# Values ahead of the turned z, and a half K tile with high and low halves one above the other

## What is computed

```python
q = (x @ Wq).reshape(b, t, h, dh).transpose(0, 2, 1, 3)      # h = 8 heads, dh = 64
k = (x @ Wk).reshape(b, t, h, dh).transpose(0, 2, 1, 3)
gl_v = (x @ Ws).reshape(b, t, h, e)                          # e = 5 experts, 2 selected
wv = _topk_mask(gl_v, SEL) * jax.nn.sigmoid(gl_v)
xv = jnp.einsum('btd,edk->btek', x, Wv)
v = jnp.einsum('bthe,btek->bhtk', wv, xv)
scores = jnp.einsum('bhid,bhjd->bhij', q * scale, k)
probs = jax.nn.softmax(scores, axis=-1)
attn = jnp.einsum('bhij,bhjd->bihd', probs, v)
mask_o = _topk_mask((x @ Wd).reshape(b, t, h, e), SEL)
out = jnp.einsum('bthe,bthk,ekd->btd', mask_o, attn, Wo)
...
x = x + jnp.tanh(g_ffn[0]) * _L0_ffn_ref(_layernorm(x, axis=-1), ...)
```

## Time and profile before

| what | us |
|---|---|
| median of 3 runs | 1264.33 (1263.65 to 1264.37) |
| the profiled execution | 1264.03 |
| its span, first to last instruction | 1262.2 |
| PE matmul busy | 1215.5 (96%), 6376 instructions |
| PE weight loads busy | 907.1 (72%) |
| DVE busy | 835.8 (66%) |
| POOL busy | 663.0 (53%) |
| ACT busy | 648.2 (51%) |

### The profile page before, as it was taken

One profiled execution on the slowest core, in us unless ns is written; L12 is line 12 of the kernel. 1 busy time (PEld: TensorE's weight loads), 2 busy tenths in 40 slices (PEclk: granted clock), 3 DMA queues, 4 the chain that ended last, 5 costly groups with the idle time before them and its releaser, 6 DMA issues.

```text
span 1262.2 us, 19742 instructions
## 1 busy us (share of the span) xinstructions
PE 1215.5 (96%) x6376; PEld 907.1 (72%) x6376; DVE 835.8 (66%) x1526; ACT 648.2 (51%) x1423; POOL 663.0 (53%) x481
## 2 busy tenths in 40 slices
PE   5899999999999999999999999999999999999995
PEld 4688888888888888766666766767667677676654
DVE  7777777778686947464675665765755756657654
ACT  6434343434343434375556656656656655665551
POOL 2724242424243433377495594692791872963971
PEclk9899999999999999999999999999999999999998
DMA  6231314132222314300011010010010020010010
GB/s 217 100 126 42 125 42 125 63 104 79 88 91 85 104 57 146 105 1 34 1 35 66 0 66 33 0 66 33 0 66 33 0 70 30 7 59 0 17 50 34
DMA packets 40666, 75.74 MB, mean 60 GB/s; under 512 B 3712, under 2 KB 4224, under 8 KB 40640
## 3 DMA queue, kind: packets, MB, share of 16 engines
q1 hardware_dynamic: 40640, 75.42, 17.5%
HBM read 58.63 MB, written 16.78 MB: 60 GB/s over the span
## 4 chain that ended last, share of the span: by engine, by line
PE 86%; DVE 7%; POOL 3%; issue 2%; ACT 1%; DMA 0%; DVEq 0%; SPq 0%; ACTq 0%; POOLq 0%
PE ps_f L878 20%; PE ps_r L1745 11%; PE ps_o L1819 9%; PE ps_s L1806 8%; PE ps_h L878 7%; PE ps_s L1798 7%; PE ps_s L878 7%; PE ps_r L1781 5%; PE ps_r L1757 5%; DVE z L1526 2%; POOL spare L1323 2%; POOL spare L1329 2%; DVE z_tmp L1515 1%; PE ps_t L912 1%; PE ps_r L1771 1%
## 5 line engine op out<-in xcount | busy, mean ns | idle before, releaser
L1341 POOL TENSOR_TENSOR z<-z,z_tmp 128x1280 f32<-128x1280 f32 x40 | 117.0, 2926 | 200.1 <-DVE z_tmp L1515 198.0
L1495 DVE TENSOR_REDUCE nmax<-ps_s 128x1 f32<-128x512 f32 x256 | 163.9, 682 | 85.1 <-PE ps_s L1798 84.0
L1389 ACT ACTIVATE pt<-ps_s 128x512 f32<-128x512 f32 x256 | 139.3, 596 | 144.7 <-PE ps_s L1806 144.4
L1323 POOL TENSOR_TENSOR spare<-xv,pick 128x512 f32<-128x512 f32 x160 | 176.0, 1100 | 41.8 <-DVE pick L1608 28.7
L1380 ACT ACTIVATE tmp<-ps_s,nmax 128x512 f32<-128x512 f32 x256 | 174.4, 694 | 15.6 <-DVE nmax L1495 15.6
L1329 POOL TENSOR_TENSOR spare<-spare 128x512 f32<-128x512 f32 x128 | 172.4, 1347 | 10.0
L1806 PEld LDWEIGHTS ps_s<-ident,tmp 128*128 128x128 f32 x1024 | 109.5, 140 | 48.5 <-issue 40.5
L1806 PE MATMUL ps_s<-ident,tmp 128*128 128x128 f32 x1024 | 140.4, 280 | 1.3 <-ACT tmp L1380 1.3
L1798 PE MATMUL ps_s<-k,q 64*128 64x512 f32 x768 | 123.5, 426 | 3.7 <-ACT pt L1389 3.7
L1819 PE MATMUL ps_o<-pt,spare 128*64 128x512 f32 x512 | 116.9, 598 | 0.7 <-ACT pt L1389 0.7
L255 POOL TENSOR_TENSOR e_t<-e_t 128x512 fp32r<-128x512 f32 x32 | 40.8, 1302 | 142.4 <-ACT e_t L474 142.4
(11 more groups left out here) (181 smaller groups left out, 2122.2 us busy)
## 6 DMA issues: line engine op xcount, KB each, us to landing
stage<-in_x SPq DMA_DIRECT2D x32, 256.0 KB, 3.1
x_sb<-in_x SPq DMA_DIRECT2D x8, 1024.0 KB, 5.4
x_dram<-x_sb SPq DMA_DIRECT2D x32, 256.0 KB, 2.4
stage<-x_dram SPq DMA_DIRECT2D x8, 1024.0 KB, 5.8
x_sb<-x_dram SPq DMA_DIRECT2D x8, 1024.0 KB, 5.7
out_dram<-x_sb SPq DMA_DIRECT2D x32, 256.0 KB, 2.0
stage<-in_ctx_t SPq DMA_DIRECT2D x28, 256.0 KB, 3.1
stage<-in_ctx SPq DMA_DIRECT2D x28, 256.0 KB, 2.7
```

The source lines that it names most:

```text
L1323: pool.tensor_tensor(v_tmp[:] if e else acc, xv[:, :, e, :].unsqueeze(2).broadcast_to(shape), pick[:, 0, e, :, 2 * p:2 * p + 2].unsqueeze( ...
L1341: pool.tensor_tensor(zv, zv, z_tmp[:, h % 2], ALU.add).then_inc(z_pool, 1)
L1389: act.activation(pt[:, h % 4, :, t * P:(t + 1) * P], ps_s[:, n % BANKS, :].rearrange("p (k t) -> p k t", k=NT), ACT.Copy).then_inc(pt_read ...
L1495: dve.tensor_reduce(nmax[:, n:n + 1], ps_s[:, n % BANKS, :], AX_X, ALU.max, negate=True).then_inc(nmax_ready, 1)
```

## The change

Two things. First, PE's shared parts move from part 2 of a step to a new part 3, so that the values of both batches come before the shared parts of both. Second, z gets 384 columns: ACT copies its last 64 columns behind themselves (`copy_last`), so the third turned tile holds the same 64 values twice, in rows 0 to 63 and in rows 64 to 127. ACT writes the whole tile as the high half into `z_t2[:, 1]`; DVE then turns rows 64 to 127 into low halves, in place. The weights' third tile holds the high half in both places, and in its low tile the low half above zeros. So two matmuls take the place of three. Result tile 0 waits for each low half just ahead of its passes.

```diff
+    LAST = KZ - 1
+    HALF = NV - LAST * P
+    assert 2 * HALF == P
...
+        z_all = sb("z", [P, NT, KZ * P])
+        z = z_all[:, :, 0:NV]
...
-            for k in range(KZ):
-                into = passing("wo", k)
-                sp.dma_start(into, wo[k * P:k * P + into.shape[0], :]).then_inc(wo_loaded[k], 16)
+            for k in range(LAST):
+                sp.dma_start(passing("wo", 0, k), wo[k * P:(k + 1) * P, :]).then_inc(wo_loaded[k], 16)
+            for place in (0, HALF):
+                sp.dma_start(wo_raw[place:place + HALF, LAST, :], wo[LAST * P:NV, :]).then_inc(wo_loaded[LAST], 16)
...
-            pool.memset(wo2[0:SHARED, :, KZ - 1, :].bitcast(F32), 0.0).then_inc(cleared, 1)
+            pool.wait_ge(cleared, 1)
+            pool.memset(wo2[HALF:P, 1, LAST, :].bitcast(F32), 0.0).then_inc(cleared, 1)
+            pool.wait_ge(cleared, 2)
...
-                    act.activation(z_t2[:, 0, n, :], ps, ACT.Copy).then_inc(zt_hi, 1)
+                    act.activation(z_t2[:, int(n == LAST), n, :], ps, ACT.Copy).then_inc(zt_hi, 1)
+
+            def copy_last(b):
+
+                act.wait_ge(z_ready, b * 2 + 2)
+                act.activation(z_all[:, :, NV:KZ * P], z_all[:, :, NV - HALF:NV], ACT.Copy).then_inc(z_copied, 1)
...
+                        if n == TURN_Z_AT[0] - STEPS and not first:
+                            copy_last(b - 1)
                         for tile in (n, n + 1):
                             if 0 <= tile < STEPS:
                                 scores_exp(b, tile, first)
...
-                    dve.tensor_tensor(z_t2[:, 1, n, :], ps, z_t2[:, 0, n, :].bitcast(F32),
+
+                    rows, high = (slice(HALF, P), 1) if n == LAST else (slice(0, P), 0)
+                    dve.tensor_tensor(z_t2[rows, 1, n, :], ps[rows], z_t2[rows, high, n, :].bitcast(F32),
                                       ALU.subtract).then_inc(zt_lo, 1)
...
+                    if n == LAST:
+                        pe.wait_ge(z_copied, b + 1)
                     for t in range(NT):
-                        end = pe.transpose(ps[:, t * P:(t + 1) * P], z[:, t, tile_at(n):tile_at(n) + P], ident[:])
+                        end = pe.transpose(ps[:, t * P:(t + 1) * P], z_all[:, t, n * P:(n + 1) * P], ident[:])
...
-                        pe.wait_ge(zt_lo, b * KZ + KZ)
                         pe.wait_ge(w_lo["wo"], KZ)
                         pe.wait_ge(cleared, 2)
-                    every = [(k, l, r) for k in range(KZ) for l, r in PASSES]
+                    every = [(k, l, r) for k in range(LAST) for l, r in PASSES] + [(LAST, 1, 0), (LAST, 1, 1)]
                     for m in taken(every, part, parts):
                         k, l, r = every[m]
+                        if n == 0 and m % len(PASSES) == 0:
+                            pe.wait_ge(zt_lo, b * KZ + k + 1)
...
                         if n == PAIR * p + PV_AT:
                             values(b, p, first)
+                if part == 3:
                     for what in parts_at(n):
                         shared_part(b, *what, first, last)
```

More of the change, by code:

```diff
@@ L1030, in expert_attention @@
     assert NT == ND == 4 and 2 * DH == P and H * DH == D
-    SHARED = KZ * P - NV
-    def tile_at(k):
-        return min(k * P, NV - P)
+    LAST = KZ - 1
+    HALF = NV - LAST * P
+    assert 2 * HALF == P
     STEPS = H * NT
@@ L1149, in expert_attention @@
         v_tmp = v_tmp.rearrange("p (t a k) -> p t a k", t=NT, a=2)
-        z = sb("z", [P, NT, NV])
+        z_all = sb("z", [P, NT, KZ * P])
+        z = z_all[:, :, 0:NV]
         z_tmp = sb("z_tmp", [P, 2, NT, E, DH])
@@ L1203, in expert_attention @@
         z_pool = sem("z_pool")
+        z_copied = sem("z_copied")
         z_ready = sem("z_ready")
@@ L1217, in of, with own_rows, passing @@
             return dram[bass.ds(b, 1)].rearrange("o p t d -> (o p) t d")
-        def own_rows(name, k):
-            return slice(SHARED if (name, k) == ("wo", KZ - 1) else 0, P)
+        def own_rows(name, half, k):
+            return slice(0, HALF if (name, half, k) == ("wo", 1, LAST) else P)
         def weight_tile(name, half, k):
-            return weights[name][own_rows(name, k), half, k, :]
+            return weights[name][own_rows(name, half, k), half, k, :]
         wo_raw = z_tmp[:].rearrange("p a t e k -> p (a t e k)")[:, 0:KZ * D].rearrange("p (k n) -> p k n", k=KZ)
         raw = {"wk": probs, "wo": wo_raw}
-        def passing(name, k):
-            return raw[name][own_rows(name, k), k, :]
+        def passing(name, half, k):
+            return raw[name][own_rows(name, half, k), k, :]
         SPLIT_AT = {"wk": EARLY - STEPS, "wo": EXPERTS_AT[2][0]}
@@ L1243, in take_weight_lo @@
             eng.wait_ge(w_hi[name], k + 1)
-            eng.tensor_tensor(weight_tile(name, 1, k), passing(name, k), weight_tile(name, 0, k).bitcast(F32),
+            eng.tensor_tensor(weight_tile(name, 1, k), passing(name, 1, k),
+                              weights[name][own_rows(name, 1, k), 0, k, :].bitcast(F32),
                               ALU.subtract).then_inc(w_lo[name], 1)
@@ L1339, in mix_sums @@
                             pool.wait_ge(z_pool, b * POOL_SUMS + h - 1)
-                        zv = z[:].rearrange("p t (e k) -> p t e k", e=E)
+                        zv = z.rearrange("p t (e k) -> p t e k", e=E)
                         pool.tensor_tensor(zv, zv, z_tmp[:, h % 2], ALU.add).then_inc(z_pool, 1)
@@ L1361, in take_weights @@
                     if name == "wo":
-                        act.wait_ge(wo_loaded[k], 16)
+                        act.wait_ge(wo_loaded[k], 32 if k == LAST else 16)
                     elif k == 0:
                         act.wait_ge(both.wk_loaded, 16)
-                    act.activation(weight_tile(name, 0, k), passing(name, k), ACT.Copy).then_inc(w_hi[name], 1)
+                    act.activation(weight_tile(name, 0, k), passing(name, 0, k), ACT.Copy).then_inc(w_hi[name], 1)
             def normalise(b, tiles):
@@ L1469, in _ @@
             for n in range(EARLY, EARLY + STEPS):
+                if n == TURN_Z_AT[0]:
+                    copy_last(B - 1)
                 for part in range(2):
@@ L1512, in mix_product @@
                 ps = ps_r[:, bank_of(("turn_o", p)), :].rearrange("p (t a k) -> p t a k", t=NT, a=2)
-                out = z_tmp[:, h % 2] if h else z[:].rearrange("p t (e k) -> p t e k", e=E)
+                out = z_tmp[:, h % 2] if h else z.rearrange("p t (e k) -> p t e k", e=E)
                 shape = [P, NT, E, DH]
@@ L1838, in _ @@
             for n in range(CUT - STEPS, CUT):
-                for part in range(3):
+                for part in range(4):
                     step(0, n, part, first=True)
```

## The result

The changed kernel takes 1247.7 us (median of 4 runs, 1247.3 to 1248.0), the kernel before on the same chip 1264.2. The ratio is 0.987, with an interval of 0.9853 to 0.9887. Run once more later, it took 1246.8 against 1264.75: 0.9863 (0.9849 to 0.9878). The profiled execution took 1248.0; its span is 1246.2, against 1262.2 before: 16.0 us less.

A forecast was written before the change was run, and what follows sets the result against it. PE, with 86% of the chain that ended last, bounds the kernel. 7 x (0.85 + 0.93) + 2.4 = 14.9 us off the profiled 1264.03 gives 1249.1, as a median 1249.4, 1.2% faster; range 1246.5 to 1254.5.

The forecast's parts named there:

- Values ahead of the turned z: In each of seven loop turns, PE's wait for z goes entirely: 0.85 us, bounds 0.74 and 1.17.
- The matmul: Each result tile goes from 9 matmuls to 8, 0.232 us each: 0.93 a batch of four tiles.
- rival 2: In result tiles, the removed matmul is worth only 0.15 us: 2.6 less gain, 1252.0; chance 0.05.
- The copy: ACT's copy of z's last 64 columns takes 0.4 us inside 1.23 us of idle time: cost nothing.
- Strided z, set-up: Sums and product over z rows of 384 instead of 320, and changed memset, waits, weight transfer and cast: 0.
- Rival 4: POOL's z sums in four runs cost more, slower overall from a sum of 6.5 us; chance 0.04.
- What is late next: Behind z turned 2.8 us later in the loop, copies, low halves, maxima and exponentials stay in time: about 2 us spare.
- Sum of the loop: Seven loop turns, each gaining 0.85 us by the order and 0.93 by the matmuls.
- The last batch: After the last z, products start 1.5 us earlier and four matmuls fall out, 0.93: 2.4 us gained.
- if the slow stretch keeps its length from the first product: Last batch's lower-clock stretch stays as long, counted from the products' start: gain 2.4 us, alternatives 0.9 and 4.5.

The follow-up runs named there:

- e12: Kernel before with values ahead of the turned z and a wait for each low half, still 9 matmuls a tile and no copy: 1255.3 us, ratio 0.9926.
- e2: Changed kernel with the shared parts back in part 2, the turned z ahead of the values: 1254.7 us, ratio 0.992.
- e4: Changed kernel with a ninth matmul ahead of each result tile, its output overwritten by the next: 1254.3 us, ratio 0.9924.
- e6: Changed kernel with four extra unused 448-column copies on ACT behind the new copy: 1248.15 us, ratio 0.9878.
- e3: Changed kernel with one wait for all low halves ahead of result tile 0: 1253.7 us, ratio 0.9913.
- e9: Kernel before with 48 unused identity transposes on PE during the last batch's wait for z: 1260.8 us, ratio 0.9972.
- e5: Changed kernel with 48 unused identity transposes on PE during the last batch's wait for z: 1247.9 us, ratio 0.9872.
- e7: Kernel before with result tile 0 waiting for each low half just ahead of its passes: 1260.25 us, ratio 0.9964.
- e1: Kernel before with only the shared parts moved behind the values; 9 matmuls a tile, one wait for all low halves, no copy: 1257.4 us, ratio 0.9949.
- e8: Changed kernel with eight extra unused 448-column copies on ACT behind the new copy: 1269.1 us, ratio 1.0046.

## Why the prediction was right, and where its steps were off

The forecast was 1249.4 with 14.9 us less, measured were 1247.7 and 16.5 less. No rival came. The mechanism held in the loop; the last batch was sized too small, and part of what it gained there came by the clock.

- *Values ahead of the turned z*: 0.85 a turn forecast, 0.81 measured (e12 against before). Within the whole change the order is worth 89.50 - 88.70 = 0.80 (e2 against the changed kernel). Right, and so is the reason: the wait is gone and nothing took its place.
- *The matmul*: 0.232 each, 0.93 a turn; measured 0.93 (e4) and 0.94 (e2, with everything else of the half tile). Right; rival 2 would have shown 0.6.
- *The copy*: 0.4 forecast, 0.42 measured, hidden with 0.78 left behind it, and e6 with 2.4 more still costs nothing. Right.
- *Strided z, set-up*: nothing, as forecast. Rival 4 needed a sum of 6.5; it is 2.93.
- *What is late next*: the exponentials of 14 are ready at 738.3 and PE asks at 740.4, 2.1 of spare for 2 forecast. The low halves were worked out too favourably: 0.3 of spare forecast for the last of them, -0.14 measured. They began 1.32 behind the start of the turned z where I had 1.1, they took 2.02 for the 1.89 that I had carried over from the earlier trace rows, and PE asked 0.1 earlier than I had it. This cost nothing only because of the three separate waits, which I had called worthless in the loop and which are worth 0.23 a turn (e3). Had the change kept the single wait, my 12.5 for the loop would have been 1.9 too high (7 x 1.51 = 10.6).
- *Sum of the loop*: 7 x 1.78 = 12.5 forecast, 7 x 1.74 = 12.2 measured.
- *The last batch*: 2.4 forecast, 4.0 measured. This is the mis-sized term. The two parts were right (1.5 and 0.93; the start came 1.67 earlier, four matmuls were 0.95 in e9 against e5). What failed is the step "if the slow stretch keeps its length from the first product": it did not keep it. It fell from about 4 us to 0.6, so the products gained 1.46 besides, within the bounds that I had given (0.9 to 4.5) but not at the value that I took. Of that, 0.80 comes from the closed gap (e7), and 0.66 from a clock that fell earlier in the wait: that part is luck, as far as is known.
- *Not in the sum*: the clock in the twelve matmuls at 588 (1.4 less) and the first stage (1.6 later). They nearly cancel in the first profiled pair. In the second the loads are alike, and the medians are 17.95 apart. That the first medians are 16.5 apart, 1.6 more than forecast, is therefore partly luck. In the second pair the miss is 3.

Loop -0.3, last batch +1.6, the two at the start -0.2: together 1.1 above the 14.9, and the spans differ by 16.0.

## What to carry to other kernels

Where PE has no gap, a matmul taken out was worth its share of an unbroken run of such matmuls, to 0.01 us here, and where it stands idle for an operand, work of another batch whose inputs are long there can be moved ahead of it, and the whole of that wait goes. Before counting such a move as free, list every operand that gets later behind it: here ACT had over 2.4 us to give and DVE's low halves none, and it was the finer wait (each operand just ahead of its use) that kept the latter from costing 0.23 a turn. In a tail behind a long wait, close the gaps between PE's pieces: the gap itself was 1.5, and in the executions whose clock fell late in the wait it held the products up by another 0.8 to 1.1 (8.57 to 8.66 without, 9.46 to 9.66 with it). And before a change is credited with a faster stretch, look whether the clock was the same ahead of the first instruction that the change touches.

## What was unexpected of the hardware

- In twelve waits of the same 6.07 us the clock fell to 0.50 after 1.3 to 4.4 us. When it came back went with that and with the gap behind the twelve transposes. The same instructions of the same tail took 7.67 (fall after 2.4, e1) and 9.46 (after 3.9, before).
- Transposes of an identity held the clock at 1.00: with 48 of them in the last wait, PE went into the turned z at full clock (1.50 in place of 2.79).
- Behind an idle time of 2.3 to 2.4 us, twelve matmuls took 2.40 in eight profiles and 3.8 in six. All six had also had the lower clock around 17 to 21 and 65 to 69 us, where six of the eight had the full one.
- In the loop's first turn of e8 the clock fell to 0.50 at 648.0, with no waits of PE but 0.79 and 0.65 in the 8 us ahead of it.
- The first wait for input differs by 1.9 us between profiles of kernels whose loads at the start are alike (10.4 to 12.3): as much as some of the effects studied here, so that such effects are better read from a turn of the loop than from the span.
